# Edge sorting's block fetches and destination scatters moved beside the dilated attentions

## The reference, cut to what matters

```python
x = x + halo_attention(ln(x))          # 8x8 blocks, halo 2, relative positions, 8 heads   (l0conv)
t = tokens(x)
t = t + routed_ffn(ln(t))              # gelu MLP for the best tokens of each image       (l0ffn)
x = x + dilated_attention(ln(x))       # 3x3 windows, dilations 2 and 3                   (l1conv)
# graph attention over 16384 nodes and 524288 random edges, then 4 experts by top-2 gating
h = ln(t) @ W_gat;  a_src = (h*att_src).sum(-1);  a_dst = (h*att_dst).sum(-1)
e = leaky_relu(a_src[src] + a_dst[dst])                    # for every edge
alpha = softmax of e over the edges of one dst
agg = segment_sum(h[src] * alpha, dst)
scores = layernorm(agg + b_gat).mean over heads;  top 2 of 4 experts, softmax
out = t + sum over experts of g[e] * (gelu(ln(t) @ W1[e] + b1[e]) @ W2[e] + b2[e])
```

## Time and profile before

| | before |
|---|---|
| median of 3 runs | 7333.31 us (7291.48 to 7333.96) |
| the profiled execution | 7323.2 us, span 7321.3 us |
| mean granted TensorE clock | 0.70 |
| busy: PE, DVE, ACT, POOL | 3180.6, 3408.2, 1543.3, 2635.4 us |
| POOL transfers in the page's groups | L951 2048 at 1071 ns, L850 128 at 1140 ns, L943 128 at 1104 ns |

### The profile page before, as it was taken

How to read it: one execution, slowest core, us unless ns; L and a number is a source line. 1 busy time by engine, 2 the same in 40 slices (tenths; PEclk the granted TensorE clock), 3 DMA queues, 4 the chain that set the end, 5 groups by cost and what they waited for, 6 DMA issues and landing times.

```text
span 7321.3 us, 84797 instructions
## 1 busy us (share of the span) xinstructions
PE 3180.6 (43%) x32140; PEld 1979.4 (27%) x32141; DVE 3408.2 (47%) x6941; ACT 1543.3 (21%) x3954; POOL 2635.4 (36%) x2472
## 2 busy tenths in 40 slices
PE   0011157687997798778873122222222222222204
PEld 0011146543773485256622000000000000000104
DVE  9999965567767685845674111111111111111128
ACT  0000034321751373045410011111111111111100
POOL 0000013210000000023003777777777777777450
PEclk9965578786997798678875555655655655655657
DMA  2000040001000100010003222222222222222207
GB/s 79 0 0 0 0 167 13 22 11 29 12 2 1 38 4 1 0 28 3 2 0 42 27 32 32 32 32 32 32 32 32 32 32 32 32 32 32 63 7 247
DMA packets 259708, 227.82 MB, mean 31 GB/s; under 512 B 115005, under 2 KB 222954, under 8 KB 250282
## 3 DMA queue, kind: packets, MB, share of 16 engines
q0 software_dynamic: 78944, 29.28, 6.4%
q1 hardware_dynamic: 99786, 99.91, 4.4%
q10 hardware_dynamic: 80640, 93.86, 4.2%
HBM read 100.42 MB, written 121.39 MB: 30 GB/s over the span
## 4 chain that ended last, share of the span: by engine, by line
PE 27%; another core or an unknown queue 23%; DVE 18%; issue 16%; DVEq 7%; ACT 4%; DMA 3%; POOL 2%; ACTq 1%; SPq 0%; POOLq 0%
DVE SA_ L1308 3%; PE PSB L1160 3%; PE PSB L382 3%; DVE SA_ L1298 2%; PE PSB L527 2%; PE PSB L366 2%; PE PSB L679 2%; POOL VPAD L961 2%; DVE SA_ L583 2%; PE PSB L352 1%; DVEq L1389 1%; PE PSB L392 1%; PE PSB L661 1%; DMA VPAD<-s_TNT 1%
## 5 line engine op out<-in xcount | busy, mean ns | idle before, releaser
L951 POOL DMA_INDIRECT SA_<-s_T,GIX x2048 | 2192.7, 1071 | 657.8 <-issue 657.8
L1160 PE MATMUL PSB<-VPAD,EH 128*128 128x512 f32 x512 | 303.0, 756 | 1996.2 <-DMA VPAD<-s_TNT 1819.6
L943 POOL DMA_INDIRECT s_AEXP<-fill,SIX x128 | 141.3, 1104 | 2331.9 <-DMA fill<-s_ADT 2122.7
L899 DVE TENSOR_TENSOR XPAD<-SA_ 128x256 f32<-128x256 f32 x32 | 14.2, 443 | 1833.9 <-DMA SA_<-s_T,GIX 1779.5
L1160 PEld LDWEIGHTS PSB<-VPAD,EH 128*128 128x128 f32 x512 | 122.1, 247 | 2199.0 <-DMA VPAD<-s_TNT 1863.3
L850 POOL DMA_INDIRECT SA_<-s_SK,BLKI x128 | 146.0, 1140 | 1251.8 <-DVE BLKI L1441 978.7
L1164 PE MATMUL PSB<-SA_,EW 128*128 128x512 f32 x512 | 346.7, 826 | 345.4 <-ACT SA_ L1145 233.1
L303 ACT ACTIVATE PRX<-PSB,MX 128x144 f32<-128x144 f32 x1024 | 375.3, 379 | 417.0 <-DVE MX L224 414.2
L1412 PE MATMUL PSB<-ident,SA_ 128*128 128x128 f32 x448 | 83.3, 369 | 837.2 <-DVE SA_ L1379 575.3
L1149 ACT ACTIVATE VPAD<-PSB,PRX 128x512 f32<-128x512 f32 x128 | 87.9, 687 | 1308.3 <-remote 918.5
L1145 ACT ACTIVATE SA_<-PSB,PRX 128x512 f32<-128x512 f32 x256 | 175.9, 687 | 777.3 <-remote 431.5
(11 more groups left out here) (365 smaller groups left out, 7485.6 us busy)
## 6 DMA issues: line engine op xcount, KB each, us to landing
SA_<-s_T,GIX POOLq DMA_INDIRECT x2048
s_Y<-VPAD ACTq DMA_DIRECT2D x32, 1024.0 KB
s_R<-zero SPq DMA_DIRECT2D x96, 256.0 KB
s_R<-XPAD ACTq DMA_DIRECT2D x32, 768.0 KB
SB_<-s_Y SPq DMA_DIRECT2D x16, 1024.0 KB, 5.4
SA_<-s_Y SPq DMA_DIRECT2D x16, 1024.0 KB, 7.2
s_AEXP<-zero SPq DMA_DIRECT2D x32, 256.0 KB, 3.0
SA_<-in_x SPq DMA_DIRECT2D x16, 512.0 KB
```

Of the source, the lines that this page charges most:

```text
L951: pool.indirect_dma_start(out=n.G[:,s,c,:],out_offset=None,in_=d["T"],in_offset=IOA(ap=n.GIX[s][:,c:c+1],axis=0)).then_inc(n.gath[s],16)
L1160: pe.matmul(PSB[:,(m%4)*512:(m%4+1)*512],n.WM1[:,m//2,(m%2)*P:(m%2+1)*P],n.TNC[:,s,:],start=True,stop=True).then_inc(n.moe_h,1)
```

## The change

Four edits. The 128 block fetches are paced by `s_kv` and `s_p2` of image 0, so they run beside its dilated attention and not beside its first attention. The position work of DVE and PE moves from behind image 0's `l0conv` to behind its `l1conv`. The 28 later fetches that are paced by `s_h` take the counter of image 1 (32 higher). The scatters of images 0, 1 and 2 are paced by `s_p2` of the next image, four in each unit, so 32 run beside each of the dilated attentions of images 1, 2 and 3, where before all 96 ran beside image 3's `l0conv`; their source is loaded by three transfers (`dst_loads`), one for each image.

```diff
 def pos_pool(pool,m,n,d):
     for t in range(NT):
-        if t%2==0 and t>=8: pool.wait_ge(n.s_ao,t//2-3)
+        if t<20: pool.wait_ge(n.s_kv,t+1)
+        else: pool.wait_ge(n.s_p2,(t-20)*66//108+1)
         pool.indirect_dma_start(out=I[:,t*BLK:(t+1)*BLK],out_offset=None,in_=d["SK"],in_offset=IOA(ap=m.BLKI[:,t:t+1],axis=0)).then_inc(n.gb_ld,16)
...
     for t in range(BLOCKS):
-        if t>=4: pool.wait_ge(n.s_h,t-3)
+        if t>=4: pool.wait_ge(n.s_h,32+t-3)
...
 def edges_pool(pool,n,d,tick,V):
+    pool.wait_ge(n.np_rdy,1)
     for t in range(NT):
-        if t==0: pool.wait_ge(n.np_rdy,1); pool.wait_ge(n.ad_ld,16)
-        if t==NT-NT//IMGS: pool.wait_ge(n.ad_ld2,16)
-        if t%2==0 and 8<=t<NT-NT//IMGS: pool.wait_ge(n.s_ao,64*(IMGS-1)+t//2-3)
+        b,i=t//TILES,t%TILES
+        if b<IMGS-1:
+            if i==0: pool.wait_ge(n.ad_ld,16*(b+1))
+            pool.wait_ge(n.s_p2,72*(b+1)+9*(i//4)+2*(i%4)+1)
+        elif i==0: pool.wait_ge(n.ad_ld2,16)
         pool.indirect_dma_start(out=d["AEXP"],out_offset=IOA(ap=n.SIX[:,t:t+1],axis=0),in_=n.ADN[:,t,:],in_offset=None,bounds_check=4096*128-1,oob_is_err=False).then_inc(n.ad_sc,16)
...
+def dst_loads(sp,n,d,b):
+
+    sp.wait_ge(n.t_st,32*(b+1))
+    if b: sp.wait_ge(n.ad_ld,16*b)
+    sp.dma_start(n.ADN[:,b*TILES:(b+1)*TILES],d["ADT"].rearrange("(t p) c -> p t c",p=P)[:,b*TILES:(b+1)*TILES]).then_inc(n.ad_ld,16)
 def edges_sync(sp,n,d,SA,tick,V):
-    sp.wait_ge(n.t_st,32*(IMGS-1))
-    sp.dma_start(n.ADN[:,0:first],adt[:,0:first]).then_inc(n.ad_ld,16)
...
-            for b in range(1,IMGS): image_loads(sp,n,d,b)
+            for b in range(1,IMGS):
+                image_loads(sp,n,d,b)
+                if b>1: dst_loads(sp,n,d,b-2)
+            dst_loads(sp,n,d,IMGS-2)
...
             def image(b):
                 l0conv_dve(dve,n,PSB,b)
+                l0ffn_dve(dve,n,PSB,b,ones)
+                l1conv_dve(dve,n,PSB,b)
                 if b==0:
                     pos_dve(dve,n,PSB,m)
                     dve.drain().then_inc(n.sorted_,1)
-                l0ffn_dve(dve,n,PSB,b,ones)
-                l1conv_dve(dve,n,PSB,b)
                 gat_dve(dve,n,PSB,b)
```

More of the change, by code:

```diff
@@ L1073, in node_dve @@
     be=lambda a: a.unsqueeze(3).to_broadcast((P,NT,4,4))
-    dve.wait_ge(n.tbn_ld,16*4); dve.wait_ge(n.ad_ld,16); dve.wait_ge(n.ad_ld2,16)
+    dve.wait_ge(n.tbn_ld,16*4); dve.wait_ge(n.ad_ld,16*(IMGS-1)); dve.wait_ge(n.ad_ld2,16)
     dve.tensor_tensor(mS,n.TBN[:,:,16:20],n.ADN[:,:,:],ALU.add)
@@ L1539, in image @@
                 l0conv_pe(pe,n,PSB,ident,b)
+                l0ffn_pe(pe,n,PSB,ident,ones,b)
+                l1conv_pe(pe,n,PSB,ident,ones,b)
                 if b==0:
@@ L1542, in image @@
                     pe.wait_ge(n.sorted_,2)
-                l0ffn_pe(pe,n,PSB,ident,ones,b)
-                l1conv_pe(pe,n,PSB,ident,ones,b)
                 gat_pe(pe,n,PSB,ident,b)
```

## The result

| | before | after |
|---|---|---|
| median | 7333.64 us (7291.48 to 7334.39, 4 runs) | 7084.8 us (7080.58 to 7104.64, 4 runs) |
| the profiled execution's span | 7321.3 us | 7080.3 us |
| granted TensorE clock | 0.70 | 0.70 |

The ratio is 0.969 (95% interval 0.966 to 0.971), so 3.1% faster. The forecast was 7079 us, with 7036 to 7150 as its range.

What follows compares the result with a forecast made beforehand. The kernel was taken as one chain of stages, two l0convs lengthened by POOL transfers holding up TensorE. 7321.3 − 145.6 − 109.4 + 6 = 7072 span, 7074 with 1.9 more, plus half of a 10 us median offset: 7079 us, range 7036 to 7150.

Steps and rivals of the forecast that it cites:

- l0conv, −145.6 and −109.4: First attention: without 120 fetches image 0 saves 145.6 us; without 96 scatters image 3 falls from 395.8 to 286.4.
- l1conv, +6: Dilated attention: its 224 added transfers cost 6 us, within 0 to 22, since TensorE takes few matmuls per us there.
- The cause: In l0conv, TensorE is held up handing out instructions while POOL builds a transfer, at 1.14 to 1.21 us each.
- The position work, 0: Moved behind image 0's l1conv: 26.0 us on the path in both places, fetches landing in time, so 0.
- Image 1's load and the later fetches, 0: Load issued late has 18 us for 11; the later fetches' at most 2.8 us moves to image 1's feed-forward: 0.
- Everything else: The last 32 scatters and all behind them stay as they are: 0.
- Rival 1: In l1conv, transfers block DVE's two-input operations by 0.47 us each: +106, giving 7179 us; chance 0.06.
- Rival 2: POOL falls behind in image 0's l1conv and DVE waits at the positions: some 7105 us; chance 0.10.
- Rival 3: In l1conv, TensorE stops throughout each transfer and DVE waits: 284 to 400 us cost, about 7400 at 1.5; chance 0.04.
- Rival 4: The two l0convs stay slow for another reason, such as DMA traffic or the clock: about 7330 us; chance 0.03.

Runs made afterwards that it cites:

- experiment 6: The unaltered changed kernel run again beside the kernel before on chip C, a third chip: 7082.3 us against 7303.1, ratio 0.968.
- experiment 8: Changed kernel plus two probes of extra, unused POOL/SP work on chip C; 96 indirect POOL transfers beside image 3's l0conv: 384.6 us against 280.0.
- the second profile of the kernel before: The kernel before itself, unaltered, profiled on chip C; l0conv of images 0 to 3 took 416.6, 289.2, 287.0 and 379.2 us.
- the first probe on B: Changed kernel plus 96 plain POOL transfers, POOL fills, SP transfers and indirect POOL transfers beside l0conv of images 0 to 3, on chip B: 6836.5 us.
- experiment 3: Changed kernel with all 128 block fetches paced by image 0's value products, none beside the keys and values: 7094.5 us, ratio 0.968 to the kernel before.
- experiments 1 and 2: Changed kernel with only the scatters moved: 7212.3 us, ratio 0.986; with only the fetches and position work moved: 7187.0 us, ratio 0.981.

## Why the prediction was right

**l0conv, −145.6 and −109.4.** 426.1 to 281.0 is −145.1; 395.8 to 280.6 is −115.2. The second is 6 us more than forecast, because the mean of images 1 and 2 was the wrong goal: image 3 has no next image's load beside its opening, which takes 33 us there and 37 to 42 in images 1 and 2. In the kernel before it took 38 us, with the eight scatters that had no wait standing in it. The part from the first L382 to the last strip took 213 to 215 us in all four images. Image 1's stage took 291.0 and not 286.7, with an opening 5 us longer; in the profile of experiment 6 it was 286.4, so this is not the change's.

**l1conv, +6.** The step that was mis-sized. The stages sum to 979.2 us against 958.9 (239.2, 242.7, 238.4, 238.6), so +20 in this profile: +15 in image 0, of which 11 are the keys and values and 4 fall behind the start of the last unit, where I found no cause; +5 in image 3, where the clock of 0.70 gives 243 in quiet stages too. The forecast averaged: 2.7 matmuls per us over the stage, fewer than l0ffn. But the keys and values are not the average (80 in 16.6 us, 4.8 per us), and 20 fetches paced by `s_kv` came as one run of 16. The argument also took from the earlier trace rows that TensorE gets 6.8 matmuls per us in the stall itself. Those rows are of a pair of builds. In the run of 16 the copies of the keys, four matmuls each, start 1.4 to 4.2 us apart from 1405.0 on, which is at most 2.8 per us, less than the keys ask for. The bounds held the cost, 0 to 22. That the median came within 6 us of 7079 all the same is partly luck, since the tail was 6 us shorter and image 3's l0conv gave 6 more than forecast. The experiments say what the argument lacked: not only matmuls per us decide but how long one run of builds is. The other 204 transfers cost at most those 4 us and the 5 of image 3.

**The cause**, TensorE held up while POOL builds a transfer, was argued from the earlier trace rows; experiment 8 shows it, and narrows it to indirect transfers. The prediction had TensorE held up "in handing out instructions"; the late signals say that this is not all of it, and how they arise is open. That it depends on the chip was not foreseen at all: on B, where the kernel before took 6833 us, the changed kernel with 398 more transfers took 6833 too. At 0.07 us for each of 216 transfers the change had some 15 us to gain there by estimate; it was not measured.

**The position work, 0.** L148 behind l1conv to the next stage took 26.2 us, 26.4 before. The last fetch was issued at 1615.9, L828 started at 1637.7 without a wait. The fetches took 0.94 to 1.45 us, mean 1.03.

**Image 1's load and the later fetches, 0.** The load was issued at 1655.6 and nothing waited for it. l0ffn of image 1 with 28 fetches took 107.2 us, 108.0 before without.

**Everything else.** l0ffn of image 3 took 112.7 us, 5.7 more, with no change there; the second profile of the kernel before has a 112.7 in image 2 and the first probe on B one in image 0, most others 107 to 110. What follows the last l1conv was 6 us shorter. Together 7080.3 of span, where 7072 was forecast: +14 in l1conv, +5 in l0ffn, −1 in the l0convs (−5.7 in image 3, +4.3 in image 1), the rest in small terms.

**The rivals.** Rival 1 (DVE blocked in turn): DVE's busy time in l1conv of image 0 is 176.88 us against 176.10, and L580 took 685 ns on average. DVE lost its time waiting for PE's results. The Trainium skill (SBUF — State Buffer, "Who interferes with whom") has the second of the two block, whichever it is; in this trace only POOL did, whose fetches stretch to 1.45 us. Rival 2 (positions late): the last fetch was issued 21 us before the stage's end. Rival 3 (TensorE stopped throughout each transfer) is what l0conv comes near with bursts of eight (1.30 us each). In experiment 3 the price is about 33 us for 128, 0.26 each. As the change spreads them, it is 15 to 20 us for 224, and not 284. Rival 4 fell with experiments 1 and 2.

## What to carry to other kernels

- Put indirect transfers of POOL beside stages with few matmuls, and in short runs. On chips A, C and D runs of up to 15 (20 us) beside l1conv's units cost 0 to 9 us in a whole stage; a single run of 13 to 16 at its keys, where matmuls are denser, cost 8 to 11, and runs of 18 to 26 beside the units some 33. More transfers beside one stage are harmless if they are spread; fewer in one run are not.
- A stage's average rate hides its dense phase. The version with 28 fetches beside l0ffn and 100 beside l1conv's units (experiments 4 and 9) leaves the keys and values alone and has the best ratios, 0.965 and 0.962 of the kernel before, against 0.969 and 0.968. The two versions never ran beside each other, and the profiles give 2 to 4 us of the difference to this stage.
- When an engine stands, ask also when its earlier results reached the others. PE's gaps in experiment 3 look like missing work of PE, and are waits for engines that had waited for PE's signals.
- Compare stages at the same granted clock before a cause is sought, and repeat a comparison on another chip before a mechanism is believed general.

## What I had not expected of the hardware

- One chip of four ran the kernel before in 6833 us and not 7303 to 7341: a build beside dense matmuls cost 0.07 us there and not 1.1, and an indirect gather took 970 ns and not 1058 to 1071.
- A plain transfer issued by POOL occupied it for 0.53 us (51.17 us for 96) and an indirect one for 1.16 (111.62 for 96), and only the second touched TensorE.
- TensorE's signals, 0.01 us behind the recorded end of a matmul in quiet stages, came up to 10.8 us behind it while POOL built indirect transfers (experiment 3).
- l1conv with the same instructions took 238, 243 or 249 us at granted clocks of 0.72, 0.70 and 0.66, with no POOL work beside it.
